# The experts' low part on VectorE instead of GpSimd, with new orders on all five engines

## The reference, cut to what matters

```
p1 = einsum('bsh,eoh->bseo', nf, mlp1_weight) + mlp1_bias
g = minimum(p1[..., 0::2], 7.0)
lin = clip(p1[..., 1::2], -7.0, 7.0)
act = g * sigmoid(1.702 * g) * (lin + 1.0)
p2 = einsum('bsei,ehi->bseh', act, mlp2_weight) + mlp2_bias
combined = einsum('bseh,bse->bsh', p2, combine)
```

## Time and profile before

| what | value |
|---|---|
| median of 3 runs | 1671.89 us (1668.73 to 1673.2) |
| profiled execution, its own time | 1678.32 us |
| its span, first to last instruction | 1676.6 us |
| busy PE, DVE, ACT, POOL | 1433.3, 1263.8, 1128.8, 931.7 us |
| mean granted clock of TensorE | 0.96 |

### The profile page before, as it was taken

The page is one execution under the profiler, slowest core; times in us unless marked ns, Lnnn a source line. Parts: engine busy times, 40 slices in busy tenths (PEclk is TensorE's granted clock), DMA queues, the critical chain, the costliest instruction groups (busy, mean ns, idle before and its releaser), DMA issues.

```text
span 1676.6 us, 16143 instructions
## 1 busy us (share of the span) xinstructions
PE 1433.3 (85%) x5357; PEld 627.4 (37%) x5425; DVE 1263.8 (75%) x1565; ACT 1128.8 (67%) x1509; POOL 931.7 (56%) x483
## 2 busy tenths in 40 slices
PE   4998788877999798986999989887799988867887
PEld 1443344333444344432344434433244433422333
DVE  2875995769866996677967799665996698669952
ACT  3548764568558876367865798555865887668863
POOL 2133581378507666077642785327861676629865
PEclk9999897999999999999999999999999999979999
DMA  7110002001200101101010010110102000010000
GB/s 177 36 38 26 1 1 88 26 1 38 79 36 1 63 1 76 38 0 38 26 76 13 0 63 1 76 38 1 38 26 88 1 13 1 31 82 1 1 1 25
DMA packets 12580, 57.12 MB, mean 34 GB/s; under 512 B 1978, under 2 KB 2002, under 8 KB 8530
## 3 DMA queue, kind: packets, MB, share of 16 engines
q1 hardware_dynamic: 11682, 49.79, 8.1%
q0 software_dynamic: 816, 6.30, 1.7%
HBM read 53.98 MB, written 7.36 MB: 37 GB/s over the span
## 4 chain that ended last, share of the span: by engine, by line
PE 55%; ACT 13%; POOL 12%; DVE 10%; issue 8%; DMA 1%; POOLq 0%; DVEq 0%; SPq 0%; another core or an unknown queue 0%; ACTq 0%
PE psf L1453 12%; PE psu L1623 6%; PE psy L1608 5%; ACT L876 4%; PE psu L1726 4%; DVE st L2174 3%; PE psf L1350 3%; PE psu L1350 3%; PE psy L1701 3%; POOL gx L751 3%; POOL gate L775 2%; PE psf L1431 2%; PE psy L1475 2%; POOL alo L782 2%; DVE psu L2157 2%
## 5 line engine op out<-in xcount | busy, mean ns | idle before, releaser
L876 ACT ACT_TABLE_LOAD x250 | 320.8, 1283 | 86.8 <-PE psu L1726 30.3
L751 POOL TENSOR_TENSOR gx<-gx,sy 128x1024 f32<-128x1024 f32 x120 | 289.0, 2408 | 110.1 <-DVE sy L2191 105.9
L775 POOL TENSOR_TENSOR gate<-gate,lin 128x1024 f32<-128x1024 f32 x56 | 135.5, 2424 | 219.9 <-DVE gate L2303 148.5
L1453 PE MATMUL psf<-g1p,h2w 128*128 128x512 f16 x768 | 177.6, 379 | 9.2 <-ACT tf L943 9.0
L1075 ACT ACTIVATE da<-delta,aneg 128x512 f32<-128x512 f32 x256 | 167.2, 711 | 1.5 <-DVE st L2174 0.7
L2157 DVE TENSOR_TENSOR psu<-so,psu 128x1024 f32<-128x1024 f32 x128 | 156.5, 1223 | 7.2 <-PE psu L1570 5.6
L2174 DVE TENSOR_TENSOR_SCAN st<-da,carry,psu 128x512 f32<-128x512 f32 x128 | 156.7, 1265 | 1.5
L2174 DVE TENSOR_TENSOR_SCAN st<-da,psu 128x512 f32<-128x512 f32 x128 | 149.1, 1206 | 3.3 <-ACT da L1075 0.8
L782 POOL TENSOR_TENSOR alo<-gate,ahi 128x1024 f16<-128x1024 f32 x60 | 133.1, 2231 | 7.9 <-ACT ahi L1175 7.9
L729 POOL TENSOR_TENSOR g2p<-tf,g2p 128x512 fp32r<-128x512 f32 x64 | 83.0, 1305 | 94.0 <-ACT g2p L966 94.0
L724 POOL TENSOR_TENSOR hp<-tf,hp 128x512 f16<-128x512 f32 x64 | 74.6, 1173 | 99.4 <-ACT hp L955 99.4
(11 more groups left out here) (356 smaller groups left out, 3046.1 us busy)
## 6 DMA issues: line engine op xcount, KB each, us to landing
mw<-in_mlp_w SPq DMA_DIRECT2D x6, 2048.0 KB, 8.1
wf<-in_wf SPq DMA_DIRECT2D x7, 1024.0 KB, 6.1
mw<-in_mlp_w SPq DMA_DIRECT2D x6, 1024.0 KB, 10.1
xn<-in_x SPq DMA_DIRECT2D x8, 512.0 KB, 5.5
xr<-in_x SPq DMA_DIRECT2D x8, 512.0 KB, 3.6
out<-outc SPq DMA_DIRECT2D x8, 512.0 KB, 3.5
spill<-kept SPq DMA_DIRECT2D x3, 1030.0 KB, 4.0
back<-spill SPq DMA_DIRECT2D x3, 1030.0 KB, 5.6
```

The source lines that it names most:

```text
L751: pool.tensor_tensor(out, chunk(gx, c), sy[:, n % 2], ALU.add).then_inc(y_acc.sem, 1)
L775: pool.tensor_tensor(gate_at(x), gate_at(x), lin_at(b, x)[:], ALU.mult).then_inc(af_done.sem, 1)
L876: act.preload_act_table_set(name)
L1453: last = pe.matmul(banks[m], w[:, t, cols], src[:, half, t], start=(t == 0 and half == 0), stop=(t == KF - 1 and half == 1))
```

## The change

Three things, which don't alter what is computed:

1. `expert_low` leaves the POOL program and enters the DVE program, word for word but for the engine. There are 64 such calls. The wait for `kept_out` goes along.
2. POOL's lists lose the 64 calls, and DVE's lists gain them, between the clips and scales of later experts.
3. The lists of POOL, ACT, PE and DVE are written anew in `opening`, `turn` and `closing`. The calls are the same, in another order. SP's list stays.

```diff
-            def expert_low(b, x):
-                if x == 2 and not tail(b):
-
-                    pool.wait_ge(kept_out.sem, kept_out.at(b, 1))
-                pool.wait_ge(ahi_done.sem, ahi_done.at(b, x + 1))
-                pool.tensor_tensor(low_at(x)[:], gate_at(x), high_at(b, x)[:], ALU.subtract)\
-                    .then_inc(alo_done.sem, 1)
...
+            def expert_low(b, x):
+                if x == 2 and not tail(b):
+
+                    dve.wait_ge(kept_out.sem, kept_out.at(b, 1))
+                dve.wait_ge(ahi_done.sem, ahi_done.at(b, x + 1))
+                dve.tensor_tensor(low_at(x)[:], gate_at(x), high_at(b, x)[:], ALU.subtract)\
+                    .then_inc(alo_done.sem, 1)
```

DVE's list of stretch A (`turn`), before and after:

```diff
-                head_norm(row, 1); expert_scale(row, 0); expert_clip(row, 0); head_z0(row, 1); expert_clip(row, 1)
-                head_z1(row, 1); expert_scale(row, 1); head_parts(row, 1); head_softplus(row, 1)
-                expert_clip(row, 2); expert_scale(row, 2); head_late(row, 1); expert_clip(row, 3)
-                expert_scale(row, 3); expert_scale(row, 4); expert_clip(row, 4); expert_clip(row, 5)
-                expert_scale(row, 5); expert_clip(row, 6); expert_scale(row, 6); expert_clip(row, 7)
-                expert_scale(row, 7); expert_sum(row, 0); ffn_task(row + 1, 0, 0); state_input(row, 1, 0)
...
+                run(weights0, 4); block_out(row, 0); run(weights0, 8); expert_parts(row, 0); head_norm(row, 1)
+                expert_clip(row, 0); expert_scale(row, 0); expert_clip(row, 1); head_z0(row, 1)
+                expert_low(row, 0); head_z1(row, 1); expert_scale(row, 1); head_parts(row, 1); expert_clip(row, 2)
+                expert_scale(row, 2); expert_low(row, 1); expert_clip(row, 3); expert_scale(row, 3)
+                head_softplus(row, 1); head_late(row, 1); expert_low(row, 2); expert_scale(row, 4)
+                expert_clip(row, 4); expert_scale(row, 5); expert_clip(row, 5); expert_low(row, 3)
+                expert_clip(row, 6); expert_scale(row, 6); expert_low(row, 4); expert_clip(row, 7)
+                expert_scale(row, 7); expert_low(row, 5); expert_low(row, 6); expert_low(row, 7)
+                expert_sum(row, 0); ffn_task(row + 1, 0, 0); state_input(row, 1, 0); ffn_task(row + 1, 0, 1)
```

DVE's new list of stretch B, from the first expert to the state stretch:

```diff
+                expert_scale(row, 8); expert_scale(row, 9); lb_scale(row + 1, 0, wave); expert_clip(row, 9)
+                lb_center(row + 1, 1, wave); expert_scale(row, 10); expert_clip(row, 10); expert_low(row, 8)
+                lb_scale(row + 1, 1, wave); expert_clip(row, 11); head_center(row + 1, 0); expert_low(row, 9)
+                expert_low(row, 10); expert_scale(row, 11); expert_clip(row, 12); block_out(row, 1)
+                expert_clip(row, 13); head_norm(row + 1, 0); expert_scale(row, 12); expert_low(row, 11)
+                expert_scale(row, 13); head_z0(row + 1, 0); expert_scale(row, 14); expert_clip(row, 14)
+                expert_low(row, 12); head_z1(row + 1, 0); expert_low(row, 13); expert_scale(row, 15)
+                expert_clip(row, 15); head_parts(row + 1, 0); expert_low(row, 14); head_softplus(row + 1, 0)
+                expert_low(row, 15); head_late(row + 1, 0); expert_sum(row, 1); ffn_task(row + 1, 1, 0)
```

DVE's new list in `closing`, the first half:

```diff
+                expert_clip(b, 1); expert_scale(b, 0); expert_scale(b, 1); state_input(b, 1, 0)
+                expert_scale(b, 2); expert_clip(b, 2); expert_low(b, 0); state_scan(b, 1, 0); expert_low(b, 1)
+                state_output(b, 1, 0); state_input(b, 1, 1); expert_clip(b, 3); expert_scale(b, 3)
+                state_scan(b, 1, 1); expert_scale(b, 4); expert_clip(b, 4); state_input(b, 1, 2); expert_low(b, 2)
+                expert_low(b, 3); state_scan(b, 1, 2); expert_scale(b, 5); state_output(b, 1, 2)
...
+                lf_center(b, 0); state_scan(b, 1, 5); state_input(b, 1, 6); expert_low(b, 5); state_scan(b, 1, 6)
+                lf_scale(b, 0); state_output(b, 1, 6); state_input(b, 1, 7); state_scan(b, 1, 7); expert_low(b, 6)
```

PE's end of each expert stretch in `turn`, before and after (stretch A, then B):

```diff
-                expert_down(row, 4); expert_down(row, 5); ffn_half(row + 1, 0, 0, 0); ffn_half(row + 1, 0, 1, 1)
-                ffn_half(row + 1, 0, 1, 0); expert_down(row, 6); expert_down(row, 7); spread_b(row, 1, 0)
+                expert_down(row, 4); ffn_half(row + 1, 0, 0, 0); expert_down(row, 5); expert_down(row, 6)
+                expert_down(row, 7); ffn_half(row + 1, 0, 1, 0); ffn_half(row + 1, 0, 0, 1)
...
-                expert_down(row, 14); ffn_half(row + 1, 1, 0, 0); ffn_half(row + 1, 1, 0, 1); expert_down(row, 15)
+                expert_down(row, 12); expert_down(row, 13); expert_down(row, 14); ffn_half(row + 1, 1, 0, 0)
+                expert_down(row, 15); ffn_half(row + 1, 1, 0, 1); ffn_half(row + 1, 1, 1, 1)
```

More of the change, by code:

```diff
@@ L815, in turn @@
[L815 to L819, removed]
@@ new lines, in turn @@
+                hidden2(row, 0, 5); head_mean(row, 1); hidden2(row, 0, 6); hidden2(row, 0, 7); head_var(row, 1)
+                expert_up(row, 0, 0); expert_turn(row, 0); expert_spread(row, 0); expert_up(row, 0, 1)
+                expert_up(row, 1, 0); expert_up(row, 1, 1); head_delta0(row, 1); expert_up(row, 2, 0)
+                head_delta1(row, 1); expert_spread(row, 1); head_bc(row, 1); expert_up(row, 2, 1)
+                expert_up(row, 3, 0); expert_down(row, 0); expert_spread(row, 2); expert_up(row, 3, 1)
@@ new lines, in turn @@
+                ffn_half(row + 1, 0, 14, 1); spread_c(row, 1, 10); ffn_half(row + 1, 0, 15, 1)
+                spread_b(row, 1, 11); ffn_half(row + 1, 0, 16, 1); ffn_half(row + 1, 0, 16, 0)
+                spread_b(row, 1, 12); spread_c(row, 1, 11); ffn_half(row + 1, 0, 17, 0)
+                ffn_half(row + 1, 0, 17, 1); ffn_half(row + 1, 0, 18, 0); spread_c(row, 1, 12)
+                ffn_half(row + 1, 0, 19, 0); spread_b(row, 1, 13); ffn_half(row + 1, 0, 18, 1)
+                spread_c(row, 1, 13); spread_b(row, 1, 14); ffn_half(row + 1, 0, 19, 1)
@@ new lines, in turn @@
+                expert_up(row, 14, 0); expert_spread(row, 13); head_delta0(row + 1, 0); expert_spread(row, 14)
+                expert_down(row, 10); expert_up(row, 15, 0); head_delta1(row + 1, 0); expert_spread(row, 15)
+                expert_up(row, 15, 1); expert_down(row, 11); head_bc(row + 1, 0); ffn_half(row + 1, 1, 1, 0)
+                expert_down(row, 12); expert_down(row, 13); expert_down(row, 14); ffn_half(row + 1, 1, 0, 0)
+                expert_down(row, 15); ffn_half(row + 1, 1, 0, 1); ffn_half(row + 1, 1, 1, 1)
@@ L1857, in turn @@
-                spread_c(row + 1, 0, 10)
+                ffn_half(row + 1, 1, 13, 0); spread_c(row + 1, 0, 8); spread_b(row + 1, 0, 9)
+                ffn_half(row + 1, 1, 13, 1); ffn_half(row + 1, 1, 14, 0); ffn_half(row + 1, 1, 15, 0)
+                ffn_half(row + 1, 1, 14, 1); spread_c(row + 1, 0, 9); spread_b(row + 1, 0, 10)
+                ffn_half(row + 1, 1, 15, 1); spread_c(row + 1, 0, 10); ffn_half(row + 1, 1, 16, 0)
+                ffn_half(row + 1, 1, 16, 1)
                 if not last:
@@ L1903, in _ @@
+                expert_spread(b, 15); expert_down(b, 12); expert_up(b, 15, 1); hidden2(b, 1, 5)
+                expert_down(b, 13); hidden1(b, 1, 7); expert_down(b, 14); expert_down(b, 15); hidden2(b, 1, 6)
+                hidden2(b, 1, 7)
             pe.wait_ge(mean_const, MEAN_CONST)
```

650 lines of the change are left out of this document (307 added, 343 removed).

## The result

The changed kernel takes 1698.4 us (median of four runs, 1698.0 to 1699.2), the kernel before 1672.6 (median of four): a ratio of 1.0164, 95% interval 1.0151 to 1.0177. The ratios in this document come with the runs and differ a little from the quotient of two medians (here 1.0155). Where two kernels are subtracted and it matters, both are given. The prediction was 1679, with 1655 to 1694 as its range. The direction was right, the size was not: +26 us, and not +7.

The account below looks back on a forecast made before the run. It took POOL to limit Stretch A, PE Stretch B, and DVE the closing's first half. Its terms, −6 + 6 + 10 − 1 − 2 = +7 us on the plain runs' 1671.9, gave 1679 us, range 1655 to 1694.

Parts of the forecast that it names:

- What bounds it: Limits by place: POOL in Stretch A, PE in Stretch B and the closing's second half, DVE in its first half.
- The low part on DVE: One low part on DVE: 1.22 us undisturbed, bounds 0.69 and 1.37, longer where it and a POOL instruction exclude each other.
- Stretch A: Expert stretch profiled at 306 to 360 us, three times: −2 us each, bounds −5 and +3, sum −6.
- my own sign of being wrong: The forecast would be wrong if Stretch A got shorter by 4 us or more.
- Stretch B: Second expert half of each turn, three times: +2 us each, bounds −1 and +5.
- the +6 of my sum: Stretch B, three times +2 us, as it entered the forecast's sum.
- Closing: End of the kernel: first half +10 us, bounds +3 and +16; second half −1, bounds −2 and +1.
- 9.8 − 3 + 4: Closing's first half: eight low parts 9.8 us, less 3 of idle filled, plus 4 of blocking, some +10.
- The reordering elsewhere: Opening, hidden and state stretches: neighbours exchanged, no instruction added or removed; −2 us for all, bounds −9 and +9.
- My own sign for this: The forecast would be wrong if hidden and state stretches changed by more than 3 us each.
- POOL's relief wins: Low parts fall between products: Stretch A −5 three times, Stretch B −1 three times, closing +3; −15, 1657 us; chance 0.35.
- Blocking everywhere: 64 low parts wait some 2 us: Stretch A 0, Stretch B +5 three times, closing +16; +29, 1701 us; chance 0.12.

Follow-up runs that it names:

- light low part on POOL: Kernel before, same places and waits, but POOL fills the low part with zeros instead of subtracting: 1663.5 us (0.9945).
- light low part on DVE: Changed kernel, same places and waits, but DVE subtracts the float16 high part from itself, leaving out the low part's value: 1677.4 us (1.0023).
- its rung: Changed kernel with the state stretches' orders and the whole closing of the kernel before, the closing's low parts on POOL: 1673.4 us (1.0000).
- the ladder: Runs from the kernel before to the changed one, each adding one more part of the change: 1672.6, 1665.8, 1665.4, 1673.4, 1685.8, 1698.4 us.
- the two halfway kernels: Mostly new orders with the low part on POOL, 1743.5 us; mostly old orders with the low part on DVE, 1732.9 us; neither pure.

## Why the prediction was wrong

**What bounds it** was read right. A is bound by POOL (light low part on POOL: −3.4 at the same clock), B isn't (0), and DVE bounds the closing (light low part on DVE: −6.3).

**The low part on DVE**: 1.22 us taken, median 1.22. The mean was said to be 1.6 to 2.0 and was 1.43; the maximum above 3 was 3.37. DVE's busy time rose by 81 us (78 to 110 said). POOL's fell by 111, not 142. Its products took 15 us of the difference: each can have to wait for a low part that came first. One such place in the changed kernel's timeline, DVE, then POOL:

```profile
333.35 2.15 DVE L2302 TENSOR_TENSOR alo<-gate,ahi 128x1024 f16<-128x1024 f32 x1
```

```profile
329.75 7.97 POOL L775 TENSOR_TENSOR gate<-gate,lin 128x1024 f32<-128x1024 f32 x3
```

Three products in a row take 7.97 us instead of 7.1, and the low part, which starts under the second of them, 2.15 instead of 1.22: it waits for that one, and the third for it. The shared lock of the Trainium skill ("SBUF — State Buffer", "SBUF: two separate sides") is borne out by these rows. It matters less than I had it: of the 64 low parts, 54 took 1.23 us or less.

**Stretch A**, −2 each: measured −4.1, −2.9, −1.9. The size is right at the same clock (−1.9); the first turn passes my own sign of being wrong (4 us or more), and 2.2 of its 4.1 us are the clock, which no term of mine had. What comes back to it, the Silu that waits for a half behind the last `expert_down`, I had inside the −2; it stands behind the sum, at 1.8 us, so at the same clock A and its state's start together gain nothing. The next limit I had wrong: I put PE there, with DVE at some 23 us in 30.3, and DVE has 28.06 with PE at 23.97. **Stretch B**, +2 each: measured −1.6, −1.4, −1.4, just outside its bound of −1. What I had counted as a cost, `head_late` behind the last low parts, was none there: it no longer stands beside a working POOL and takes 1.41 us, where the earlier trace rows has 3.16.

```profile
546.44 1.23 DVE L2302 TENSOR_TENSOR alo<-gate,ahi 128x1024 f16<-128x1024 f32 x1
547.58 1.41 DVE L2127 SCALAR_TENSOR_TENSOR gx<-so,pk,gx 128x512 f32<-128x512 f32 x2
549.02 1.23 DVE L2131 TENSOR_TENSOR so<-delta,so 128x1024 f32<-128x1024 f32 x1
550.28 1.22 DVE L2311 TENSOR_SCALAR sum<-psu 128x1024 bf16<-128x1024 f32 x1
```

But its cost came behind it: in the traces of its rung the state stretch after it is 3 us longer each time, against 1.5 gained. Together with its head the new B costs 4 us there, which is close to the +6 of my sum, by another way than I had it.

**Closing**, +10 and −1: measured +11.0 and +0.2, and +12.4 by the ladder. The last state scan starts 131.9 us after the head, 121.5 before:

```profile
1611.89 2.45 DVE L2158 TENSOR_TENSOR_SCAN st<-da,carry,psu 128x512 f32<-128x512 f32 x2
```

The place and the size are right, but the two corrections in "9.8 − 3 + 4" aren't, and that they cancel is luck. The window of after that answers to 1485.4 to 1594.3 in the earlier trace rows, from 15.1 us behind the head to the end of the last scan:

```profile
1495.10:1614.30 119.20, 88.86 (x270) 33.98 (x273) 109.52 (x112) 84.18 (x104) 76.89 (x31) 0.88 0.00 0
```

DVE is busy 6.5 us more, and idle 9.7 us instead of 5.8: none of its idle time was filled, it grew, in waits for PE. And there was no blocking: each of the eight low parts in it took 1.20 to 1.23 us.

**The reordering elsewhere**, "I take −2 for all of them, bounds −9 and +9": this is the step that failed. It measured +23 in the traces: −7.9 in the opening, −1.8 in the hidden stretches, +32.7 in the six state stretches. By experiment, the state stretches' own orders are +12.6 us (+16.4 by the ratios, +18.0 in the traces) and the opening's −5.9. The other 14.7 of the 32.7 stay with the old lists in these stretches, so they come from how the new expert halves hand over; behind A that is seen (1.8 us each), behind B the seam isn't told apart from it. My own sign for this, hidden and state stretches that change by more than 3 us each, came out for the state stretches. "No row prices it" was true of any one exchange of neighbours. It was not true of the stretch: a window of the kernel before has DVE busy 81 of 83.5 us over sixteen dependent steps. Such a stretch has next to no idle time left to win (2.6 us), and every wait that a new order adds is a loss. The bounds should have been lopsided, not ±9. And I took a stretch's end as its whole worth, without asking what it leaves to the next.

**The rivals.** "POOL's relief wins" didn't come: even with nothing put on DVE, a relief of 80 us on POOL is worth 8 us in the old orders, about half of the 15 that this rival had with DVE's cost already taken off. "Blocking everywhere" gave nearly the right time, 1701, by a mechanism that isn't there: A and B got shorter, and 10 of 64 low parts waited. That its number is near is luck.

Open is which exchanges inside the state stretches cost the 12.6 us. The runs show that it is not ACT's or PE's list alone, and that the two together give back about a third; DVE's and POOL's were tried only as a pair. Single exchanges weren't tried.

## What to carry to other kernels

Where orders are worked out anew for all engines, price each stretch by what it has left: one in which an engine is busy 97% of a chain of dependent steps can hardly gain, and waits of one or two microseconds, repeated in every turn, outweigh what was won where the change was made. Measure a stretch together with the one behind it, because what the one gains may be work that it leaves to the other. Don't judge orders or an engine for a task by swapping one of them (the two halfway kernels were 60 and 70 us slower than before, the whole change 26), and look for the part that is worth keeping apart from the rest: the opening, −5.9 us, had nothing to do with the move.

## What the runs showed of the hardware

- A subtraction of a float16 tile of 128x1024 in SBUF from itself, with a float16 result, takes 0.685 us on DVE at the median, the same with one float32 input 1.22 us. The f16 form too is held up beside POOL: its maximum is 2.78 us, and POOL's products still averaged 2.49 us against 2.42.
- Filling a float16 tile of 128x1024 takes POOL 0.95 us, a subtraction of that size 2.23.
- The sixteen state steps after A took 81.3 us in every turn of the six kernels with all four old lists there (the one before among them), whatever ran ahead of them. With the new lists they took 85.3, 84.4 and 83.7 us in the three turns, and 81.5, 85.0 and 81.5 with the light low part: the same instructions in the same orders, entered a little differently. The longest have the lowest mean granted clock: 0.92, 0.92 and 0.96, and 0.96, 0.90 and 0.96 with the light low part. Which of the two brings the other wasn't followed up.
- The mean granted clock of stretch A was 0.94, 0.97 and 1.00 in the three turns of the kernel before, for 60.9, 59.7 and 58.7 us, and again so (60.9, 59.8, 58.7 us) with the new opening ahead of it. In the windows of the kernel before PE is busy 51.08, 49.16 and 47.91 us there, for the same 191 matmul records.
